# The last stage of a GNN and mixture-of-experts kernel: gates in four parts, six of seven batches mixed on TensorE, one batch loaded early

## The reference

```python
h = (x_flat @ W_gat).reshape(M, HEADS, NUM_EXPERTS)
e = leaky_relu(a_src[src] + a_dst[dst])
alpha = softmax of e over the edges of one dst
agg = segment_sum(h[src] * alpha, dst) + b_gat
scores = _layernorm(agg, ln_gamma, ln_beta).reshape(M, HEADS, NUM_EXPERTS).mean(1)
topk_s, topk_i = jax.lax.top_k(scores, TOP_K)          # two of four experts
w = jax.nn.softmax(topk_s, axis=-1)
for ei in range(NUM_EXPERTS):
    g = where(topk_i == ei, w, 0.0).sum(-1)            # the gate of a node for expert ei
    out = out + g[..., None] * (gelu(x @ W1[ei] + b1[ei]) @ W2[ei] + b2[ei])
x = x + out
```

## Time and profile before

| | |
|---|---|
| time, median of 3 runs | 2653.91 us (2652.13 to 2655.37) |
| time of the profiled execution | 2654.01 us |
| its span | 2652.3 us |
| busy: VectorE | 1942.4 us (73%) |
| busy: TensorE matmul | 1803.9 us (68%) |
| busy: GpSimd | 1706.8 us (64%) |
| busy: ScalarE | 654.5 us (25%) |

### The profile page before, as it was taken

One profiled execution on the slowest core, in us unless ns is written; L12 is line 12 of the kernel. 1 busy time (PEld: TensorE's weight loads), 2 busy tenths in 40 slices (PEclk: granted clock), 3 DMA queues, 4 the chain that ended last, 5 costly groups with the idle time before them and its releaser, 6 DMA issues. The chain is left out here.

```text
span 2652.3 us, 26078 instructions
## 1 busy us (share of the span) xinstructions
PE 1803.9 (68%) x7567; PEld 1395.6 (53%) x7567; DVE 1942.4 (73%) x3764; ACT 654.5 (25%) x1404; POOL 1706.8 (64%) x1760
## 2 busy tenths in 40 slices
PE   3731443356545454666566999999999899999316
PEld 2421112244434343344345778888888788888215
DVE  7788786998868788767676757766776566676338
ACT  6820001123222222132232521111211121211023
POOL 0000577777777777777754777777777777777560
PEclk9865776678777776888787899999999899999658
DMA  5130316567666666576667731222222222221358
GB/s 164 49 30 0 109 28 192 187 215 256 215 206 215 197 215 204 175 244 204 213 210 262 184 87 40 57 48 48 48 48 60 40 54 50 48 48 41 117 221 318
DMA packets 153561, 354.46 MB, mean 134 GB/s; under 512 B 55192, under 2 KB 96014, under 8 KB 143778
## 3 DMA queue, kind: packets, MB, share of 16 engines
q1 hardware_dynamic: 69707, 200.22, 21.2%
q0 software_dynamic: 69056, 120.72, 19.4%
q10 hardware_dynamic: 14714, 32.61, 3.2%
HBM read 180.36 MB, written 172.06 MB: 133 GB/s over the span
## 5 line engine op out<-in xcount | busy, mean ns | idle before, releaser
L620 POOL DMA_INDIRECT at_ring<-table,e_col x744 | 710.2, 955 | 226.7 <-issue 226.7
L2180 POOL DMA_INDIRECT at_ring<-table,at_idx x693 | 680.0, 981 | 211.1 <-issue 210.8
L2272 PE MATMUL at_psS<-at_ring,at_hot 128*128 128x260 f32 x1584 | 440.6, 442 | 93.0 <-DVEq L2378 85.5
L2272 PEld LDWEIGHTS at_psS<-at_ring,at_hot 128*128 128x128 f32 x1584 | 322.1, 219 | 203.0 <-issue 81.0
L1607 PE MATMUL ffn_psH<-xnT,ffn_space 128*128 (+1 forms) x896 | 362.3, 547 | 0.3 <-ACT ffn_space L1674 0.3
L1620 PE MATMUL ffn_psY<-ffn_space 128*128 128x256 f32 x1568 | 356.8, 380 | 0.0
L2294 ACT ACTIVATE at_ring<-at_psS 128x520 f32<-128x520 f32 (+1 forms) x432 | 237.6, 567 | 462.0 <-PE at_psS L2272 462.0
L887 DVE SCALAR_TENSOR_TENSOR pick_prod<-const_iota,pick_tile,pick_rows 128x400 f32<-128x400 f16 x280 | 164.0, 627 | 237.2 <-PE pick_rows L867 228.8
L1620 PEld LDWEIGHTS ffn_psY<-ffn_space 128*128 128x128 f32 x1568 | 298.4, 190 | 53.5 <-issue 13.4
L1607 PEld LDWEIGHTS ffn_psH<-xnT,ffn_space 128*128 128x128 f32 x896 | 268.1, 311 | 47.6 <-issue 1.8
L1674 ACT ACTIVATE ffn_space<-ffn_psH,ffn_b 128x448 f32<-128x448 f32 x224 | 129.7, 630 | 658.5 <-PE ffn_psH L1607 658.4
(11 more groups left out here) (427 smaller groups left out, 2488.4 us busy)
## 6 DMA issues: line engine op xcount, KB each, us to landing
at_sums<-at_ring SPq DMA_DIRECT2D x72, 1452.0 KB, 6.1
products<-ffn_space ACTq DMA_DIRECT2D x28, 512.0 KB
late_space<-products SPq DMA_DIRECT2D x28, 512.0 KB, 10.6
at_ring<-table,e_col POOLq DMA_INDIRECT x843, 2.8
at_sums<-at_ring SPq DMA_DIRECT2D x16, 768.0 KB, 3.3
at_ring<-table,at_idx POOLq DMA_INDIRECT x693, 3.1
products<-ffn_space ACTq DMA_DIRECT2D x28, 384.0 KB
late_space<-products SPq DMA_DIRECT2D x28, 384.0 KB, 13.6
```

What stands on the lines that cost most here:

```text
L620: g.indirect_dma_start(self.ring[z][:, k, 0:TW], None, self.table, bass.IndirectOffsetOnAxis(ap=self.runs.col[:, u * U + k:u * U + k + 1], ...
L2180: g.indirect_dma_start(self.ring[z][:, k, 0:self.TW], None, self.table, bass.IndirectOffsetOnAxis(ap=self.idx[:, z, k:k + 1], axis=0)).the ...
L2272: last = pe.matmul(self.psS[at % 2][:, k - lo, 0:TW], self.hot[:, b, k, :], rows[:, b * self.SUB + k, 0:TW], start=True, stop=True)
```

## The change

Six edits:

1. `Collect.bring` loses its bounds check, in both layers (98 gathers).
2. The patch is scattered after 8 gathers instead of 14, and `mend` is issued by ScalarE's queue, behind `col.scalar`, instead of by SyncE's, behind 24 loads.
3. x and the products of batch 0 are loaded by ScalarE's queue, as soon as the last product is stored, before ScalarE computes the last unit's exponents. SyncE's queue loads batches 1 and 2 at the point where it loaded x and batches 0 to 2.
4. The gates are computed in four parts, of 14, 14, 14 and 7 tiles. VectorE adds batches 0 and 1 between part 1 and part 2 and does all else behind part 3.
5. TensorE mixes batches 0, 1, 2, 3, 4 and 6, VectorE weighs batch 5 alone. VectorE finishes them in the order 0, 1, 2, 3, 5, 4, 6. ScalarE's diagonals and its pieces of the gates are interleaved anew.
6. The last batch's rows are stored in two pieces (4 tiles, then 2).

```diff
     def bring(self, g, t):
         g.indirect_dma_start(self.acc[:, t, :], None, self.att.sums,
-                             bass.IndirectOffsetOnAxis(ap=self.runs.end_idx[:, t:t + 1], axis=0),
-                             bounds_check=self.att.sums.shape[0] - 1, oob_is_err=False).then_inc(self.s_acc[t // BATCH], 16)
+                             bass.IndirectOffsetOnAxis(ap=self.runs.end_idx[:, t:t + 1], axis=0)).then_inc(self.s_acc[t // BATCH], 16)
...
-    BY_PE, ORDER = (0, 1, 2, 4), (0, 1, 3, 2, 5, 4, 6)
+    BY_PE, ORDER = (0, 1, 2, 3, 4, 6), (0, 1, 2, 3, 5, 4, 6)
...
-    def begin(self, sp, ffn, s_done):
+    def begin(self, a, ffn):
+        ffn.all_kept(a)
+        a.dma_start(self.x[:, :, :], self.x_dram).then_inc(self.s_in, 16)
+        for half in range(2):
+            self.bring(a, 0, half)
+
+    def fill(self, sp, ffn, s_done):
         ffn.all_kept(sp)
         sp.wait_ge(s_done, 1)
-        sp.dma_start(self.x[:, :, :], self.x_dram).then_inc(self.s_in, 16)
-        for i in range(self.R):
+        for i in range(1, self.R):
             for half in range(2):
                 self.bring(sp, i, half)
...
-                              ln_beta, W1.shape[0], (range(0, 3), range(3, 7)), spread.seed[:, :, :].rearrange("p j h -> p (j h)"))
+                              ln_beta, W1.shape[0], (range(0, 2), range(2, 4), range(4, 6), range(6, 7)), spread.seed[:, :, :].rearrange("p j h -> p (j h)"))
...
-                        mix.begin(sp, ffn, pick.s_done)
-                        col.mend(sp)
+                        mix.fill(sp, ffn, pick.s_done)
                         mix.sync(sp)
...
                         for t in range(T):
-                            if t == 2 * BATCH:
+                            if t == BATCH + 1:
                                 col.patch(g)
                             col.bring(g, t)
...
-                        gates.vector(v, 0)
-                        v.sem_inc(mix.s_gates, 1)
-                        gates.vector(v, 1)
-                        v.sem_inc(mix.s_gates, 1)
-                        for i in Mix.ORDER:
-                            if i in Mix.BY_PE:
-                                mix.add(v, i)
-                            else:
-                                mix.weigh(v, i)
+                        for part, added in enumerate(((), Mix.ORDER[0:2], (), Mix.ORDER[2:])):
+                            gates.vector(v, part)
+                            v.sem_inc(mix.s_gates, 1)
+                            for i in added:
+                                if i in Mix.BY_PE:
+                                    mix.add(v, i)
+                                else:
+                                    mix.weigh(v, i)
```

More of the change, by code:

```diff
@@ L1813, in add, with put, store @@
                 .then_inc(self.s_v, 1)
-    def store(self, a, i):
-        B, full = BATCH, self.N // P
-        a.wait_ge(self.s_v, self.done[i])
-        lo, hi = i * B, min((i + 1) * B, full)
+    def put(self, a, lo, hi):
+        hi = min(hi, self.N // P)
         a.dma_start(self.out_dram[lo * P:hi * P, :].rearrange("(t p) d -> p t d", p=P), self.x[:, lo:hi, :])\
             .then_inc(self.s_out, 16)
+    def store(self, a, i):
+        a.wait_ge(self.s_v, self.done[i])
+        self.put(a, i * BATCH, (i + 1) * BATCH)
     def end(self, a):
-        full = self.N // P
+        i, full = self.ORDER[-1], self.N // P
+        assert i in self.BY_PE and i == self.batches - 1 and self.HALVES[1][0] == self.PAIRS[1][1]
+        for (lo, hi), pairs in zip(self.HALVES, (2, len(self.PAIRS))):
+            a.wait_ge(self.s_v, self.done[i] - len(self.PAIRS) + pairs)
+            self.put(a, i * BATCH + lo, i * BATCH + hi)
         if full < self.T:
             a.dma_start(self.out_dram[full * P:self.N, :], self.x[0:self.N - full * P, full, :]).then_inc(self.s_out, 16)
-        a.wait_ge(self.s_out, 16 * (self.batches + (full < self.T)))
+        a.wait_ge(self.s_out, 16 * (self.batches + 1 + (full < self.T)))
     def weigh(self, v, i):
@@ L2964, in _ @@
                             ffn.store(a, 0, i - ffn.LAG - 1)
+                        mix.begin(a, ffn)
                         att.exponents(a, att.units - 1)
                         col.scalar(a)
+                        col.mend(a)
                         gates.scalar(a, 0)
@@ L2974, in _ @@
                         gates.expert_weights(a, 1)
-                        mix.diagonals(a, 2, 0, 0)
+                        mix.diagonals(a, 2, 1, 0)
+                        gates.self_weights(a, 2)
                         mix.store(a, 0)
-                        mix.diagonals(a, 2, 0, 1)
+                        mix.diagonals(a, 2, 1, 1)
+                        gates.deviations(a, 2)
                         mix.store(a, 1)
-                        mix.diagonals(a, 4, 1, 0)
-                        mix.diagonals(a, 4, 1, 1)
-                        for i in Mix.ORDER[2:]:
-                            mix.store(a, i)
+                        mix.diagonals(a, 3, 1, 0)
+                        gates.expert_weights(a, 2)
+                        mix.diagonals(a, 3, 1, 1)
+                        gates.self_weights(a, 3)
+                        mix.diagonals(a, 4, 2, 0)
+                        gates.deviations(a, 3)
+                        gates.expert_weights(a, 3)
+                        mix.diagonals(a, 4, 2, 1)
+                        mix.store(a, 2)
+                        mix.diagonals(a, 6, 3, 0)
+                        mix.store(a, 3)
+                        mix.diagonals(a, 6, 3, 1)
+                        mix.store(a, 5)
+                        mix.store(a, 4)
                         mix.end(a)
```

## The result

| | before | after |
|---|---|---|
| median | 2653.91 us (5 runs, 2650.68 to 2656.49) | 2640.67 us (5 runs, 2638.40 to 2643.58) |
| span of the profiled execution | 2652.3 us | 2636.7 us |

The ratio is 0.9952, with a 95% interval of 0.9939 to 0.9966: 13.2 us faster. The profiled execution of after took 2638.4 us, 2.3 less than its median. Three executions of the experiments, all on one chip (4539 us in e2, 6685 in e3, 10068 of before), took far longer than the others of their kernel and are left out of every median and ratio. I compare medians for the size of the gain and rows for its place.

A forecast was written before the change was run, and what follows sets the result against it. GpSimd's edge gathers were taken as the bound ahead, VectorE behind S0. S0 at 2532.4 plus 110 us behind it gave a span of 2642.4; with execution time 1.7 above span, 2644 us, range 2637 to 2653.

The forecast's parts named there:

- check, 49 gathers ahead of the edge gathers: First layer, GpSimd: dropping the bounds check saves 0.054 us a gather, bringing everything behind forward by 2.6 us.
- issue of nine DMAs hidden on ScalarE: Early load of x and batch 0: ScalarE issues it before it is next wanted at 2497.5, costing no issue time.
- g: Start of the last edge gather on GpSimd, from which traces are compared; forecast from the old trace's 2491.4.
- S0: Moment VectorE starts the gates: 2556.6 before, forecast at 2532.4, 24.2 us earlier.
- TensorE's gap: After four batches TensorE idles some 9 us until VectorE's add of batch 2 frees its banks.
- cost of its restart at the lower clock: TensorE's clock falls during its wait for the add of batch 2; its next matmuls lose 1.7 us.
- the fast copy: Copy of mended before the gates: on ScalarE's empty queue it lands in 5.5 us, not SyncE's 14.5.
- free check: Rival at the gathers of sums: removing the bounds check gives nothing; 2647 us, chance 0.12.
- slow copy: Rival before the gates: copy of mended takes 14.5 us in ScalarE's queue too; 2652.5 us, no change, chance 0.11.
- milder contention: Rival: last edge gather lands as before and TensorE keeps its clock, -2.9 and -1.7 us; 2639 us, chance 0.11.
- the peak of the transfers: Rival: last edge gathers meet x's transfer, landing in 14.2 us instead of 5.2; +9 us, 2653 us, chance 0.06.
- The other side: Rival: small DMAs meet peak transfers everywhere, S0 is 2553.4, the stage behind 14.3 us longer; 2662 us, slower, chance 0.10.

The follow-up runs named there:

- e2: Changed kernel with the copy of mended issued by SyncE behind 16 loads, run on the slower chip: 3935.86 us, 1.0078 of the kernel before there.
- e7: Changed kernel with early load, earlier patch and ScalarE's issue of the copy all undone, other edits kept: 2662.24 us, 1.0042 of the kernel before.
- e5: Kernel before the change with only the patch behind 8 gathers and the copy of mended on ScalarE's queue: 2654.90 us, 1.0004 of before.
- e2b: Changed kernel with the copy of mended issued by SyncE behind the loads of batches 1 and 2: 2641.45 us, 0.9954 of the kernel before.
- e3c: Changed kernel without the early load; SyncE loads x and batches 0 to 2, ScalarE keeps the copy: 2643.61 us, 0.9960 of the kernel before.
- e6: Kernel before the change with only the bounds check removed from the gathers of sums: 2651.98 us, 0.9992 of before.
- e4c: Changed kernel with VectorE's add of batch 2 moved between the third and fourth part of the gates: 2634.63 us, 0.9921 of the kernel before.
- e1: Changed kernel with the bounds check back on the gathers of sums, run on the slower chip: 3917.16 us, 1.0044 of the kernel before there.
- e4: Changed kernel with the add of batch 2 between the gates' third and fourth part, on the slower chip: 3913.62 us, 1.0028 of before there.

## Why the prediction was right, step by step

The forecast was 2644 us (2637 to 2653), faster. Measured were 2640.67 us.

| step | predicted | measured in after |
|---|---|---|
| check, 49 gathers ahead of the edge gathers | 2.6 us | 2.7 (mean of six kernels without, two with) |
| issue of nine DMAs hidden on ScalarE | yes | yes, 19.2 us idle behind them |
| landing of the last edge gather | 5.2 | 6.3 |
| g to the first gather of sums | 22.4 | 23.4 |
| patch landing, copy landing | 5.2, 5.5 | 5.7, 4.4 |
| g to S0 | 43.6 | 43.8 |
| part 0; part 1 with its waits | 15.7; 21.7 | 15.3; 21.1 |
| last part with its waits | 15.4 | 13.7 |
| TensorE's gap | 9 | 8.39 |
| cost of its restart at the lower clock | 1.7 | 3.05 |
| last add to the end | 5.6 | 5.5 |
| S0 to the end | 110 | 108.6 |

**The start of the gates.** Right in sum, and each term within 1.1 us: the last gather landed 1.1 us later than charged, and the copy 1.1 us sooner. The direct sums are 2.6 + 21.6 us predicted and 2.7 + 21.4 measured.

**The reason for the fast copy** was only half the truth. I wrote that the 14.5 us is the landing of SyncE's queue when full, and that ScalarE's queue is empty by then. Both hold (e7: 14.4 us; e5: 7.0 where SyncE's loads took 13.5 and more). But the step left out that edit 3 alone empties SyncE's queue in time: e2b has the same 4.4 us without the other queue, and without the emptier queue it would have been nearer 7 (e5, e3c). That the time came out with the 5.5 us is in part luck.

The Trainium skill (DMA: Bandwidth & Descriptors, Issuing engines are not separate DMA queues) says that a second issuing engine saves only issue time. The traces don't agree where SyncE's queue is long: there the copy in ScalarE's queue took 7.0 us (e5) and 6.7 (e3c) while SyncE's loads took 13.5 to 15.6. They agree between e2b and after, where SyncE's queue is short: 4.4 us in either.

**The stage behind S0.** The last part took 13.7 us and not 15.4: a fixed part of 10.5 us and 0.37 a tile, read from parts of 21 and 28 tiles, was too dear for 7 tiles. That and the parts ahead, which ended about 1 us early, brought the add of batch 2 2.2 us forward (75.2 us after S0 instead of 77.4, its own 2.1 us being 2.4). TensorE then gave 1.35 us of it back, as its restart took 3.05 us and not 1.7. I had the 1.7 from a single row; the first matmuls after the long idle took 8.65 us in after, 8.87 in before and 9.85 in e6. The sum is 1.4 us shorter than predicted.

The 6 us that part 1 loses were forecast as a wait for ScalarE alone. In after 2.11 us of them are a wait for sums, which I had not seen; e7, where the sums are there, loses 6.39 us to ScalarE instead. So ScalarE's diagonals set the end of this wait, as forecast, and the wait for sums cost nothing more. Two slips in the working have no effect on the sum: the add of batch 0 comes out at 39.5 us and not 40.5 (15.7 + 15.7 + 6 + 2.1), hidden behind TensorE either way, and VectorE's own work grows by 2.9 us (21.0 - 22.3 + 4.2) where I called it the same.

**The rest of the difference.** Spans differ by 15.6 us where I forecast 9.9. In after the first gather of sums, in layer one, starts at 1419.2, 4.6 us earlier than before, and no edit stands ahead of it. It is variation between executions: the other kernels without the check had it at 1418.9 to 1424.6. With the 1.4 us of the stage, less 0.2 at S0, that is the whole of it, to 0.1 us. The medians, 13.2 us apart, hold less of it, but some: the terms above give 11.2 us (2.7 + 21.4 - 12.9).

**The rivals.** The free check is refuted (e6's median). The slow copy did not come, since the two halves of the change each prevent it. The milder contention did not come either: the last gather landed 4.0 us later than before, 1.1 more than charged. Neither did the peak of the transfers: the last gather took 6.3 us and not 14.2, the patch 5.7 and not 10. The other side, that the stage behind S0 has become longer and loses when S0 isn't 14.3 us early, is real, and e7 measures it: 12.7 us longer. Edits 2 and 3 had to be undone for it to show; contention did not do it.

## What to carry to other kernels

Two groups of edits of which one gives nothing alone (e5) and the other costs 9.7 us alone (e7) can gain together: an earlier start is worth what the next supply lets through (here gathers at 1.25 us a tile). Before splitting such work, read what its second part waits for.

A consumer that frees a buffer (here an add that frees PSUM banks) belongs ahead of a long independent piece in its own engine's order, when another engine waits for the buffer: moving one add gave 6 us, nearly half as much as the whole change.

An issue that is hidden on an engine is hidden by idle time at that place. Name how much (19.2 us here), and what happens when the stage ahead shifts so that it is gone.

## What was unexpected of the hardware

- A copy of 588 KB took 14.4 to 14.5 us behind 24 loads of its own queue (before, e6, e7). In another queue, with 13 of these loads issued and 11 following, it took 6.7 to 7.0 us while the loads beside it took 13.5 to 15.6 (e5, e3c). With only 16 loads ahead it took 4.1 to 4.4 us in either queue (after, e4c, e2b; in e2b the last load was issued 9.9 us before it).
- The same wait of TensorE, 8.39 or 8.40 us at the same point of the program, was followed by first matmuls of 10.12 us (after), 10.18 (e7), 8.88 (e2b) and 8.95 (e3c) instead of 7.07: the restart from the lower clock level cost 1.8 to 3.1 us in executions of nearly the same program.
- A bounds check adds 0.052 us to an indirect gather on GpSimd (e5 and e6, one chip) and 0.050 on the slower chip (e1 and e4).
- One chip ran these kernels some 1250 us slower. There the last edge gather started 112 us ahead of the last store of products instead of behind it (e4), and none of the variants of the change was faster than before.
